# One half of a GRU state update rewritten as candidate plus gate times the difference

## What is computed

```python
def cell(h, x):
    gi = x @ W_ih + b_ih
    gh = h @ W_hh + b_hh
    i_r, i_z, i_n = jnp.split(gi, 3, axis=-1)
    h_r, h_z, h_n = jnp.split(gh, 3, axis=-1)
    r = jax.nn.sigmoid(i_r + h_r)
    z = jax.nn.sigmoid(i_z + h_z)
    n = jnp.tanh(i_n + r * h_n)
    h_new = (1.0 - z) * n + z * h
    return (h_new, h_new)
_, hs = jax.lax.scan(cell, initial_state, xs)      # 256 steps, one after the other
```

## Time and profile before

| | us |
|---|---|
| median of 3 runs | 2099.68 |
| lowest and highest run | 2096.22, 2102.19 |
| profiled execution, its own time | 2096.19 |
| span of that execution, first to last instruction | 2094.3 |

### The profile page before, as it was taken

One profiled execution on the slowest core, in us unless ns is written; L12 is line 12 of the kernel. 1 busy time (PEld: TensorE's weight loads), 2 busy tenths in 40 slices (PEclk: granted clock), 3 DMA queues, 4 the chain that ended last, 5 costly groups with the idle time before them and its releaser, 6 DMA issues. The chain is left out here.

```text
span 2094.3 us, 86137 instructions
## 1 busy us (share of the span) xinstructions
PE 1870.1 (89%) x32542; PEld 1374.3 (66%) x32542; DVE 1266.1 (60%) x5543; ACT 1083.5 (52%) x4105; POOL 374.2 (18%) x1398
## 2 busy tenths in 40 slices
PE   7877898999999899999877999989898989999876
PEld 4234364554645446364656888989898989888775
DVE  6454473636637365473244677767777777777766
ACT  0343636446363663637534555656565655555444
POOL 3000000000000000000001333333333333333335
PEclk7788999999999999999987797969796979889556
DMA  5122204132131322203223000000000000000002
GB/s 195 66 65 71 82 6 115 44 81 77 30 98 31 87 72 57 84 4 76 76 51 107 1 1 0 0 0 0 0 0 0 0 0 0 0 0 0 0 0 81
DMA packets 103527, 86.76 MB, mean 41 GB/s; under 512 B 15616, under 2 KB 90496, under 8 KB 103440
## 3 DMA queue, kind: packets, MB, share of 16 engines
q1 hardware_dynamic: 101392, 84.38, 14.0%
q10 hardware_dynamic: 1664, 1.18, 0.2%
q0 software_dynamic: 384, 0.01, 0.0%
HBM read 60.20 MB, written 21.00 MB: 39 GB/s over the span
## 5 line engine op out<-in xcount | busy, mean ns | idle before, releaser
L1257 PE MATMUL bank_pair_A<-moving,rep 128*128 128x16 f16 x8192 | 329.0, 172 | 69.3 <-ACT bank_pair_C L1340 40.8
L1257 PEld LDWEIGHTS bank_pair_A<-moving,rep 128*128 128x128 f16 x8192 | 268.7, 99 | 107.6 <-DVE moving L1482 80.7
L1257 PE MATMUL bank_pair_C<-moving,rep 128*128 128x16 f16 x8192 | 321.9, 171 | 0.0
L1257 PE MATMUL bank_pair_B<-moving,rep 128*128 128x16 f16 x8192 | 321.9, 171 | 0.0
L1257 PEld LDWEIGHTS bank_pair_B<-moving,rep 128*128 128x128 f16 x8192 | 266.3, 99 | 0.0
L1257 PEld LDWEIGHTS bank_pair_C<-moving,rep 128*128 128x128 f16 x8192 | 266.2, 99 | 0.0
L1349 ACT ACTIVATE r_gate<-r_pre 128x8 f32<-128x8 f32 (+1 forms) x512 | 110.5, 216 | 293.0 <-DVE r_pre L1442 256.4
L1244 PE MATMUL bank_pair_D<-x_part,w_in 128*128 128x256 f16 x1536 | 208.5, 283 | 7.6 <-ACT gi_rz L1377 5.0
L1442 DVE TENSOR_REDUCE r_pre<-bank_pair_A 128x8 f32<-128x16 f32 (+1 forms) x512 | 97.9, 191 | 138.5 <-PE bank_pair_A L1257 120.1
L1137 POOL TENSOR_TENSOR x<-x,w_in 128x512 f32<-128x512 f32 x8 | 10.2, 1274 | 958.5 <-DMA w_in<-w_in 958.5
L1043 DVE TENSOR_REDUCE head_max<-bank_pair_A 128x2 f32<-128x1024 f32 x128 | 155.8, 1217 | 35.6 <-PE bank_pair_A L579 35.4
(11 more groups left out here) (256 smaller groups left out, 3532.7 us busy)
## 6 DMA issues: line engine op xcount, KB each, us to landing
rep<-parts SPq DMA_DIRECT2D x256, 64.0 KB
parts<-parts SPq DMA_DIRECT2D x48, 256.0 KB, 2.1
q_rep<-parts SPq DMA_DIRECT2D x32, 256.0 KB, 4.9
k_rep<-parts SPq DMA_DIRECT2D x64, 128.0 KB, 2.9
w_in<-in_x_dram SPq DMA_DIRECT2D x8, 512.0 KB, 4.4
x<-in_x_dram SPq DMA_DIRECT2D x8, 512.0 KB, 4.2
parts<-parts SPq DMA_DIRECT2D x32, 128.0 KB, 2.6
out_dram<-res SPq DMA_DIRECT2D x16, 256.0 KB, 2.0
```

What stands on the lines that cost most here:

```text
L1257: last = nc.tensor.matmul(ps[part][:, o:o + 2 * B], w[:, k, (first + c) * P:(first + c) * P + P], moving[:, k, :, :].rearrange("p s b -> p ...
```

## The change

Part 1's new state is computed in another form: `apart` takes HS-scaled old state minus HS times the candidate (into `z_old`), `moved` multiplies it with the gate z (into `z_new`), and `new_state(1)` adds HS times the candidate. `kept` and `taken` are left to part 0. On VectorE `apart` stands between `new_state(0)` and `lo_part(0)`, `moved` where `kept(1)` and `taken(1)` stood. The number of VectorE instructions in a step, 18, stays. Part 0's arithmetic stays.

```diff
                 def kept(part):
-                    dve.wait_ge(z_ok, step * 2 + (part + 1))
-                    nc.vector.tensor_tensor(z_old[:, SLICE[part], :], z_gate[:, SLICE[part], :], old[:, SLICE[part], :], ALU.mult).then_inc(zh_ok, 1)
+                    dve.wait_ge(z_ok, step * 2 + 1)
+                    nc.vector.tensor_tensor(z_old[:, SLICE[0], :], z_gate[:, SLICE[0], :], old[:, SLICE[0], :], ALU.mult).then_inc(zh_ok, 1)
...
                 def taken(part):
 
-                    if part == 0:
-                        dve.wait_ge(n_ok, step * 2 + 1)
...
+                    dve.wait_ge(n_ok, step * 2 + 1)
...
+                def apart():
+                    dve.wait_ge(n_ok, step * 2 + 2)
+                    nc.vector.scalar_tensor_tensor(out=z_old[:, SLICE[1], :], in0=cand[:, SLICE[1], :], scalar=-HS,
+                                                   in1=old[:, SLICE[1], :], op0=ALU.mult, op1=ALU.add).then_inc(zh_ok, 1)
+
+                def moved():
+                    dve.wait_ge(z_ok, step * 2 + 2)
+                    dve.wait_ge(zh_ok, step * 2 + 2)
+                    nc.vector.tensor_tensor(z_new[:, SLICE[1], :], z_gate[:, SLICE[1], :], z_old[:, SLICE[1], :], ALU.mult).then_inc(zn_ok, 1)
+
                 def new_state(part):
                     dve.wait_ge(zn_ok, step * 2 + (part + 1))
+                    scale, of, to = ((-HS, z_new, z_old), (HS, cand, z_new))[part]
                     for out, done in ((moving[:, SLICE[part], 0, :], hi_done), (new[:, SLICE[part], :], st_ok)):
-                        nc.vector.scalar_tensor_tensor(out=out, in0=z_new[:, SLICE[part], :], scalar=-HS, in1=z_old[:, SLICE[part], :],
+                        nc.vector.scalar_tensor_tensor(out=out, in0=of[:, SLICE[part], :], scalar=scale, in1=to[:, SLICE[part], :],
                                                        op0=ALU.mult, op1=ALU.add).then_inc(done, 1)
...
                 new_state(0)
+                apart()
                 lo_part(0)
-                kept(1)
-                taken(1)
+                moved()
                 new_state(1)
                 lo_part(1)
```

More of the change, by code:

```diff
@@ L1463, in kept @@
                 def kept(part):
-                    dve.wait_ge(z_ok, step * 2 + (part + 1))
-                    nc.vector.tensor_tensor(z_old[:, SLICE[part], :], z_gate[:, SLICE[part], :], old[:, SLICE[part], :], ALU.mult).then_inc(zh_ok, 1)
+                    dve.wait_ge(z_ok, step * 2 + 1)
+                    nc.vector.tensor_tensor(z_old[:, SLICE[0], :], z_gate[:, SLICE[0], :], old[:, SLICE[0], :], ALU.mult).then_inc(zh_ok, 1)
                 def taken(part):
-                    if part == 0:
-                        dve.wait_ge(n_ok, step * 2 + 1)
-                    nc.vector.scalar_tensor_tensor(out=z_new[:, SLICE[part], :], in0=z_gate[:, SLICE[part], :], scalar=1.0,
-                                                   in1=cand[:, SLICE[part], :], op0=ALU.subtract, op1=ALU.mult).then_inc(zn_ok, 1)
+                    dve.wait_ge(n_ok, step * 2 + 1)
+                    nc.vector.scalar_tensor_tensor(out=z_new[:, SLICE[0], :], in0=z_gate[:, SLICE[0], :], scalar=1.0,
+                                                   in1=cand[:, SLICE[0], :], op0=ALU.subtract, op1=ALU.mult).then_inc(zn_ok, 1)
+                def apart():
[6 more added lines that the diff above has]
+                    nc.vector.tensor_tensor(z_new[:, SLICE[1], :], z_gate[:, SLICE[1], :], z_old[:, SLICE[1], :], ALU.mult).then_inc(zn_ok, 1)
                 def new_state(part):
                     dve.wait_ge(zn_ok, step * 2 + (part + 1))
+                    scale, of, to = ((-HS, z_new, z_old), (HS, cand, z_new))[part]
                     for out, done in ((moving[:, SLICE[part], 0, :], hi_done), (new[:, SLICE[part], :], st_ok)):
-                        nc.vector.scalar_tensor_tensor(out=out, in0=z_new[:, SLICE[part], :], scalar=-HS, in1=z_old[:, SLICE[part], :],
+                        nc.vector.scalar_tensor_tensor(out=out, in0=of[:, SLICE[part], :], scalar=scale, in1=to[:, SLICE[part], :],
                                                        op0=ALU.mult, op1=ALU.add).then_inc(done, 1)
```

## The result

Four timed runs of the changed kernel gave 2114.20 to 2117.03 us, median 2115.44; four of the kernel before 2096.22 to 2102.19 us, median 2100.51. The ratio is 1.0074, with a 95% interval of 1.0058 to 1.0090: the change makes the kernel slower by about 15 us (14.9 us between the medians). Forecast were 2113.4 us and +0.65%.

The account below looks back on a forecast made before the run. The prediction took a ring of small dependent steps through ScalarE, VectorE and TensorE to bound the recurrence. 10.3 us plus 3.4 us gave +13.7 us on 2099.7 us, so 2113.4 us, range 2104 to 2122 us with the rivals.

Parts of the forecast that it names:

- a sum of +13.7 us: Over the recurrence: 156 full-clock product steps at 0.066 us plus 60 steps without product or split at 0.056 us, 0.65%.
- The chain, not TensorE, bounds the step: In each recurrence step, ScalarE gates, small VectorE instructions and TensorE form a ring; 0.06 us more per link lengthens the step equally.
- The second wait is a separate instruction and costs 0.10 us: At `moved`: the wait for `zh_ok`, written second, ends last and costs 0.10 us, against 0.03 us for one on the instruction.
- `apart` takes 0.176 us: On VectorE, part 1: `apart` runs as long as L1471, the same operation on the same 24 elements, 0.176 us.
- D: Distance from the end of part 1's candidate to the start of `new_state(1)`: 0.46 or 0.47 us before, 0.526 us forecast.
- 28 split steps cost nothing: Steps with the second half of a split of x on GpSimd: VectorE is held there, 0.01 us lost, taken as 0.
- 12 product steps hide the change: Product steps bound by TensorE at 1.2 GHz: the 0.06 us is hidden by 0.83 us.
- a rival: TensorE's slack or clock: one more slow product step costs 0.77 us, one per block 5.4 us, 2118.8 us; chance 0.07.
- The later low half of part 0 costs nothing: `apart` before `lo_part(0)` delays TensorE's first batch 0.09 to 0.10 us; of 0.14 us slack, 0.11 us are left.
- A semaphore between VectorE operations is free by the Trainium skill: At `moved`: by this rule the added wait is free; as rival 2098.2 us, chance 0.10; the prediction spoke against it.

Follow-up runs that it names:

- The kernel with the exchange: Changed kernel with the two waits of `moved` exchanged, `zh_ok` (result of `apart`) first and `z_ok` second: 2099.11 us, ratio 0.9994 to the kernel before.
- `mul_n`'s exchange: Kernel before with the two waits of `mul_n` exchanged, `r_ok` first and `n_ps` second: 2096.75 us, ratio 0.9985.

## Why the prediction was right

- **The number**: a sum of +13.7 us against 14.9 us between the medians. That it came so near is in part luck: the recurrence itself got 17.0 us longer in the traces, 3.3 us more than the sum, and the medians of four runs each show only 14.9 of it.
- **The chain, not TensorE, bounds the step**: right. Removing and adding 0.07 us on VectorE moved the step by 0.07 to 0.08 us in three kernels.
- **The second wait is a separate instruction and costs 0.10 us**: right, with its size: 0.105 us over all steps of the changed kernel, which a single row reads as 0.11. The kernel with the exchange shows the kind: 0.03 us, and 216 steps at their old length.
- **`apart` takes 0.176 us**: 0.182 us, so 0.006 us more. It was sized by L1471, an operation of the same kind and size with other operands. With 0.105 instead of 0.10 for the wait, D came out at 0.539 us instead of 0.526, and a full-clock product step grew by 0.07 to 0.08 us instead of 0.066. Over the 154 full-clock product steps and the 60 others that is about 2 us of the 3.3 by which the recurrence exceeded the sum of 13.7 us.
- **28 split steps cost nothing**: right, -0.4 us. The working in it was right too: with the second wait off the path they gained 2.2 us.
- **12 product steps hide the change**: right for each such step, but there are 14 of them in the changed kernel; two more, at 0.78 us over a full-clock step of this kernel, are +1.5 us. This was in the prediction only as a rival and as width of the range.
- **The later low half of part 0 costs nothing**: right. TensorE's first batch came 0.09 us later against the candidate; 0.14 us were left behind its last group (1301.96 + 0.20 to 1302.30), 0.11 forecast. The kernel with `moved` exchanged has the same late batch and costs nothing.
- **A semaphore between VectorE operations is free by the Trainium skill** (page VectorE: DVE Perf Modes, section The DRAIN you can't avoid): there a semaphore after every copy cost nothing over one after the last. The page doesn't measure two waits in front of one instruction. The runs here agree where the second wait ends early (ratio 0.9999); where it ends last they show 0.07 us a step (ratio 1.0092), and the measurement decides.

## What to carry to other kernels

Where an instruction has two waits, look in the trace for the one that is an instruction of its own, and write the wait that ends last so that it is not that one; here it was the one written second, and exchanging two lines was worth 16 us. Judge a change on a chain of small dependent operations by the distance from the last input to the first consumer, each link with its wait, and not by the number of operations. If the engine that is fed by such a chain runs at two clocks, as TensorE does here, a gain on the chain can be taken back there: count the steps at each clock in both traces. And look outside the changed code too: 2 us of the gain of `mul_n`'s exchange lay there.

## What the runs showed of the hardware that was not expected

- A shorter step brought more steps at the lower clock: 20 or 21 instead of 12 with product steps of 3.37 to 3.38 us. The count repeated exactly in the second trace of the three kernels that have one. A longer step also brought more (14 and 17). What sets the count was not settled.
- Eight matmuls without use, of 256 columns each, in every step without a product held the granted clock at 1.00 in those stretches of the second, fourth and eighth block, and the recurrence took 16.4 us less. With four it was 0.56 in the second block and 0.51 in the eighth, though TensorE was busy for as long (second block: 27.6 of 28.4 us, against 27.3 of 28.2 with eight and 21.5 of 28.4 with none). Even with eight, two steps ran at the lower clock in each of three of the seven product stages, behind steps at 1.00.
